# The heads' reciprocals of a three-stage language-model tower on one core: four transposes to 8 rows in place of one transpose to 32 rows and four masked copies

## What is computed

```python
h = relu(conv2(emb[ids]))                       # embedding and a two-tap filter
u = layernorm(h)
x_t = A x_(t-1) + B u_t                         # for 4 heads of 64, all t (a scan)
x = x / max_over_head(|x|) * exp(2)             # each token, each head
h = h + x @ C + u @ D
h = h + gelu(next(fc2_e(gelu(fc1_e(x_attn)))))  # x_attn = normed(h) @ attn + h, 8 experts
```

## Time and profile before

| | us |
|---|---|
| median of 3 runs | 210.72 (210.22 to 210.72) |
| span of the profiled execution, first to last instruction | 206.2 |
| PE busy | 181.0 |
| DVE busy | 143.2 |
| ACT busy | 116.5 |
| POOL busy | 97.5 |

### The profile page before, as it was taken

How to read it: one execution, slowest core, us unless ns; L and a number is a source line. 1 busy time by engine, 2 the same in 40 slices (tenths; PEclk the granted TensorE clock), 3 DMA queues, 4 the chain that set the end, 5 groups by cost and what they waited for, 6 DMA issues and landing times. The chain is left out here.

```text
span 206.2 us, 4072 instructions
## 1 busy us (share of the span) xinstructions
PE 181.0 (88%) x1407; PEld 163.3 (79%) x1407; DVE 143.2 (69%) x411; ACT 116.5 (56%) x317; POOL 97.5 (47%) x144
## 2 busy tenths in 40 slices
PE   0498999999999999999694999988979979996993
PEld 0276789999899987887594898987969969995891
DVE  1859956753444434669587685995977959569994
ACT  2037986554433355454444577847759577693771
POOL 0116644999200002239576184672843917656441
PEclk9999999999999999999999699999999999999999
DMA  5991000000000000000000000010100100010012
GB/s 137 399 423 62 3 0 5 2 0 3 0 0 3 0 0 2 3 0 0 0 3 2 0 3 0 0 51 5 51 0 3 52 0 27 27 51 2 3 52 102
DMA packets 2566, 7.60 MB, mean 37 GB/s; under 512 B 309, under 2 KB 1122, under 8 KB 2290
## 3 DMA queue, kind: packets, MB, share of 16 engines
q1 hardware_dynamic: 2258, 7.15, 9.1%
q10 hardware_dynamic: 288, 0.20, 0.4%
HBM read 5.25 MB, written 2.10 MB: 36 GB/s over the span
## 5 line engine op out<-in xcount | busy, mean ns | idle before, releaser
L421 POOL TENSOR_TENSOR hid_p<-hid_f,hid_p 128x256 fp32r<-128x256 f32 x56 | 40.2, 734 | 35.8 <-ACT hid_p L566 27.6
L564 ACT ACTIVATE hid_f<-bank,pa 128x256 f32<-128x256 f32 x64 | 30.3, 478 | 22.6 <-PE bank L1091 22.6
L1091 PE MATMUL bank<-xaT_p,fc_p 128*128 128x256 f32 x192 | 35.7, 297 | 0.8 <-ACT hid_f L564 0.7
L1111 PE MATMUL bank<-hid_p,out_hi 128*128 128x256 f32 x128 | 33.6, 288 | 0.6 <-POOL hid_p L421 0.5
L473 ACT ACTIVATE X<-bank 128x128 f32<-128x128 f32 x64 | 17.6, 279 | 23.3 <-PE bank L935 23.1
L1091 PEld LDWEIGHTS bank<-xaT_p,fc_p 128*128 128x128 f32 x192 | 27.3, 191 | 3.4 <-issue 2.0
L932 PE MATMUL bank<-uT,pa 128*128 128x128 f32 x128 | 25.1, 280 | 0.1
L843 DVE TENSOR_SCALAR xp<-h,mv,rstd 128x128 f32<-128x128 f32 x32 | 22.5, 762 | 3.3 <-POOL rstd L439 3.3
L1111 PEld LDWEIGHTS bank<-hid_p,out_hi 128*128 128x128 f32 x128 | 23.8, 188 | 1.2 <-POOL hid_p L421 0.9
L935 PE MATMUL bank<-X,pa 128*128 128x128 f32 x120 | 23.2, 275 | 0.0
L566 ACT ACTIVATE hid_p<-bank,pa 128x256 fp32r<-128x256 f32 x48 | 23.0, 478 | 0.0
(11 more groups left out here) (123 smaller groups left out, 384.4 us busy)
## 6 DMA issues: line engine op xcount, KB each, us to landing
fc_w<-in_fc SPq DMA_DIRECT2D x2, 2048.0 KB, 11.2
out<-res SPq DMA_DIRECT2D x7, 256.0 KB, 2.0
pb<-in_pack_b SPq DMA_DIRECT2D x1, 320.0 KB, 4.2
pa<-in_pack_a SPq DMA_DIRECT2D x1, 279.0 KB, 3.5
out<-res SPq DMA_DIRECT2D x2, 128.0 KB, 1.7
conv_w<-in_conv ACTq DMA_DIRECT2D x1, 128.0 KB, 3.4
pc<-in_pack_c ACTq DMA_DIRECT2D x1, 66.5 KB, 3.8
rowsel<-in_rows SPq DMA_DIRECT2D x1, 64.0 KB, 3.8
```

The lines of the kernel that those rows point to most:

```text
L421: nc.gpsimd.tensor_tensor(hid_p[1][:, half, c, :], hid_f[:, m % HID_SLOTS, :], hid_p[0][:, half, c, :].bitcast(F32), ALU.subtract).then_in ...
L564: full = nc.scalar.activation(hid_f[:, m % HID_SLOTS, :], src, ACT.Gelu, bias=bias)
L1091: last = mm(bank[5 + n % 2][:, 0:HALF], fc1_p[w][:, e * HID + c * P:e * HID + (c + 1) * P], xaT_p[m][:, b % 2, half, :], start=(k == 0), s ...
L1111: last = mm(out_bank(b, half)[:, half * HALF:(half + 1) * HALF], out_p[w][:, e, c * CH:(c + 1) * CH], hid_p[m][:, half, c, :], start=(c == ...
```

## The change

`r_s` gets the order (block, part, head) instead of (part, block, head), so that the 8 numbers of a block lie side by side. Each block is transposed by itself to 8 rows, into its own 128 columns of bank 4. Bank 4 then holds 8 rows by 512 columns, with no entry that has to be zeroed, and ACT takes it over with one plain copy. Before, one transpose gave 32 rows by 128 columns, and ACT wrote them four times, each time with a mask (`tile`, a scale for each partition) that kept the rows of one block. `sel_r` has 8 rows instead of 32, and the mask leaves `pack_c`.

```diff
-PC_COLS = dict(ident=P, iota=1, tile=NQ)
+PC_COLS = dict(ident=P, iota=1)
...
-        rcp = sb("rcp", [P, 2, NQ * NH])
-        r_s = sb("r_s", [P, 2, NS, NQ * NH])
-        r_T = sb("r_T", [NS * NQ * NH, 2, L], F32R)
+        rcp = sb("rcp", [P, 2, NQ, NH])
+        r_s = sb("r_s", [P, 2, NQ, NS, NH])
+        r_T = sb("r_T", [NS * NH, 2, L], F32R)
...
-        bank_rt = bank[4][0:NS * NQ * NH, 0:P]
+        bank_rt = bank[4][0:NS * NH, :]
...
-                            for q in range(NQ):
-                                mask = pc[0:NS * NQ * NH, PC["tile"]][:, q:q + 1]
-                                last = nc.scalar.activation(r_T[:, b % 2, q * P:(q + 1) * P], bank_rt, ACT.Copy,
-                                                            scale=mask)
-                            last.then_inc(rT_ready, 1)
+                            nc.scalar.activation(r_T[:, b % 2, :], bank_rt, ACT.Copy).then_inc(rT_ready, 1)
...
-                        hi = r_s[:, b % 2, 0, :]
-                        chained(nc.vector.tensor_scalar(hi.bitcast(F32R), rcp[:, b % 2, :], E2, None, ALU.mult))
-                        nc.vector.scalar_tensor_tensor(out=r_s[:, b % 2, 1, :], in0=rcp[:, b % 2, :], scalar=E2,
+                        hi = r_s[:, b % 2, :, 0, :]
+                        chained(nc.vector.tensor_scalar(hi.bitcast(F32R), rcp[:, b % 2], E2, None, ALU.mult))
+                        nc.vector.scalar_tensor_tensor(out=r_s[:, b % 2, :, 1, :], in0=rcp[:, b % 2], scalar=E2,
...
-                    nc.tensor.transpose(bank_rt, r_s[:, b % 2, :, :].rearrange("p s n -> p (s n)"),
-                                        ident).then_inc(rt_done, 1)
+                    for q in range(NQ):
+                        last = nc.tensor.transpose(bank_rt[:, q * P:(q + 1) * P],
+                                                   r_s[:, b % 2, q].rearrange("p s n -> p (s n)"), ident)
+                    last.then_inc(rt_done, 1)
```

More of the change, by code:

```diff
@@ L105, in build @@
         pb = sb("pb", [P, PB_N])
-        sel_r = sb("sel_r", [NS * NQ * NH, NP * P], F32R)
+        sel_r = sb("sel_r", [NS * NH, NP * P], F32R)
         fc1_p = [sb(f"fc1_p{s}", [P, NE * HID], F32R) for s in range(NS)]
@@ L182, in build @@
             attn_g = sb_early("attn_g", [P, CH])
-            sel_f = sb_early("sel_f", [NS * NQ * NH, NP * P])
+            sel_f = sb_early("sel_f", [NS * NH, NP * P])
         hid_p = [sb(f"hid_p{s}", [P, 2, HC, HALF], F32R) for s in range(NS)]
@@ L761, in _ @@
                         dve.wait_ge(amax_ready, b + 1)
-                        chained(nc.vector.reciprocal(rcp[:, b % 2, :],
-                                                     amax[:, b % 2, :, :].rearrange("p q n -> p (q n)")))
+                        chained(nc.vector.reciprocal(rcp[:, b % 2], amax[:, b % 2]))
                         if b >= 2:
                             dve.wait_ge(rt_done, b - 1)
-                        hi = r_s[:, b % 2, 0, :]
-                        chained(nc.vector.tensor_scalar(hi.bitcast(F32R), rcp[:, b % 2, :], E2, None, ALU.mult))
-                        nc.vector.scalar_tensor_tensor(out=r_s[:, b % 2, 1, :], in0=rcp[:, b % 2, :], scalar=E2,
+                        hi = r_s[:, b % 2, :, 0, :]
+                        chained(nc.vector.tensor_scalar(hi.bitcast(F32R), rcp[:, b % 2], E2, None, ALU.mult))
+                        nc.vector.scalar_tensor_tensor(out=r_s[:, b % 2, :, 1, :], in0=rcp[:, b % 2], scalar=E2,
                                                        in1=hi, op0=ALU.mult, op1=ALU.subtract).then_inc(rs_ready, 1)
@@ L1193 @@
     pack_b = np.concatenate([parts[n] for n in PB_COLS], 1)
-    tile = np.zeros((P, NQ), np.float32)
-    rows = tile[:NS * NQ * NH].reshape(NS, NQ, NH, NQ)
-    sel = np.zeros((NS, NQ, NH, NP, 2, DH), np.float32)
-    for q in range(NQ):
-        rows[:, q, :, q] = 1
+    sel = np.zeros((NS, NH, NP, 2, DH), np.float32)
     for n in range(NH):
-        sel[:, :, n, n // 2, n % 2, :] = 1
-    pack_c = np.concatenate([np.eye(P, dtype=np.float32), np.arange(P, dtype=np.float32)[:, None], tile], 1)
+        sel[:, n, n // 2, n % 2, :] = 1
+    pack_c = np.concatenate([np.eye(P, dtype=np.float32), np.arange(P, dtype=np.float32)[:, None]], 1)
     arrays = dict(
         ids=ids, emb=f(L0_tok_emb_weight), conv=f(L0_tok_conv_weight)[:, 0, :].T.reshape(1, 2 * CH),
-        pack_a=pack_a, pack_b=pack_b, sel=sel.reshape(NS * NQ * NH, NP * P),
+        pack_a=pack_a, pack_b=pack_b, sel=sel.reshape(NS * NH, NP * P),
         pack_c=pack_c, rows=np.repeat(np.eye(2 * NB, dtype=ml_dtypes.bfloat16), P, 1),
```

## The result

Over 20 runs of each, the changed kernel takes 211.22 us and the one before 210.47 (medians). The ratio is 1.0076, with a 95% interval of 1.0042 to 1.0110. The ratio gives + 1.6 us on 210.47, with + 0.9 to + 2.3 inside the interval: slower by about 1%, where + 1.9 was forecast. The runs of one kernel spread by more than the change is worth (208.07 to 211.80 and 209.70 to 214.78).

What follows compares the result with a forecast made beforehand. Rounds were taken as bound by two rings through PE's work after the reciprocals' transpose. Batches 2 to 7 + 1.98, batch 1 + 0.33, batch 0 - 0.38 give + 1.93 us: 212.6 us, whole range 211.2 to 213.7.

Steps and rivals of the forecast that it cites:

- The three transposes: Three added PE transposes per batch, taken as 0.11 us apart like other float32 ones: 0.33 us a batch.
- Four copies to one: ACT's copies of 1.11 us become one of 0.60, `r_T` ready 0.18 sooner; worth nothing from batch 1 on.
- Batch 0: The one place where the copies are on the path: L884 starts 0.38 us sooner, so - 0.38.
- Both rings: Dependency loops closing a round, over DVE and over POOL, both through PE after the reciprocals' transpose; each 0.33 us longer.
- The ring over DVE: Loop from the transpose of `r_s` over the transposes of `xa`, ACT's copy and DVE to the next `r_s`; 0.33 longer.
- the hold: DVE's L769 takes 0.70 us instead of 0.18 while POOL's subtraction runs, delaying `r_s` by 0.52; expected to stay.
- the copies release `xaT_p`: Rival: `xaT_p` waits for ACT's copies, so 0.18 us sooner in seven batches; - 1.6 us, 209.1; chance 0.05.
- the hold goes away: Rival: DVE's L769 is no longer slowed by POOL, saving up to 2.3 us, 210.3; chance 0.12.
- the other ring: Loop from the transpose over PE's matmuls, ACT's `hid_p` and POOL's subtraction, which slows DVE's L769; expected 0.33 us longer.
- From span to median: The 4.5 us between the profiled span of 206.2 and the median were taken to stay after the change.
- new holds: Rival: two more passes of DVE's L769 are slowed by POOL, 0.52 us each; + 1.0, 213.7; chance 0.11.

Runs made afterwards that it cites:

- experiment 1: Kernel before with its transpose of the reciprocals issued four times instead of once, the four masked copies kept; 1.0136 times the kernel before.
- experiment 2: Kernel before with one transpose and one unmasked copy of 32x512 in place of four masked copies, masking left out; 0.9943 times the kernel before.
- experiment 3: Changed kernel with its one copy of 8x512 cut into four plain copies of 8x128; 1.0082 times the kernel before.
- experiment 9: Kernel before with one more, unneeded matmul of 128x256 on PE in each of rounds 0 to 3; 0.9958 times the kernel before.
- experiment 10: Changed kernel with one more, unneeded matmul of 128x256 on PE in each of rounds 0 to 3; 1.0048 times the kernel before.
- experiment 8: Kernel before with one plain copy of 32x128 for four masked ones, and eight spreading matmuls of 128 columns for two of 512; 0.9954 times the kernel before.
- second profile: The changed kernel run again without any edit, on the same chip as the kernel before; 1.0080 times the kernel before, span 208.4 us.
- experiment 5: Changed kernel with 16 unread identity transposes filling PE's idle time before batch 3's wait for `r_s`; 1.0059 times the kernel before.

## Why the prediction was right

**The three transposes: right.** 0.11 us apart was taken; four take 0.60 us with 0.27 for one, (0.60 - 0.27) / 3 = 0.11. The eight weight columns make no difference: experiment 1 with 32 columns has 0.60 to 0.61 (and 1.01 once, in the window of the fallen clock). With the 56 ns of the Trainium skill, page "TensorE: Matmul & The Clock Gate", section "Wait — 56ns, not 53.3ns?", the sum would have been + 0.8 us, an estimate that lies just outside the measured + 0.9 to + 2.3. The rounds say 0.33 clearly.

**Four copies to one: right.** The copy takes 0.59 where 0.60 was taken. Its gain is nothing from batch 1 on (experiments 2 and 3). The price of the mask is now known: four copies of 128 columns take 1.11 us with it (32 rows) and 0.74 without (8 rows), 0.09 each. The Trainium skill, page "ScalarE: Activation LUTs", section "What ACT_TABLE_LOAD costs", gives about 93 ns for each per-partition operand (a scale or a bias with one value for each partition), and the runs agree.

**Batch 0: right.** The chain there was read from three rows. In the changed kernel:

```profile
76.94 0.60 PE L1014 MATMUL bank<-pc,r_s 128*8 128x128 f32 x4
...
77.58 0.59 ACT L575 ACTIVATE r_T<-bank 8x512 fp32r<-8x512 f32 x1
...
78.27 1.13 PE L878 MATMUL bank<-pb,fc_w 128*128 128x128 f32 x8
```

L878 comes 1.33 us behind the first transpose, against 1.72: - 0.39, where - 0.38 was forecast. It is carried whole to batch 1 (- 0.40).

**Both rings get longer by 0.33: right.** + 0.31 to + 0.33 in five intervals, and + 0.2 to + 0.3 from batch 7's transpose to the end of the span. The ring over DVE alone, without the hold, goes from 13.03 and 13.05 to 13.33 (experiments 9 and 10). PE's waits before batches 2 and 3 are 1.85 and 2.80 as before: idle time that was no cushion.

**Rival, the copies release `xaT_p`: refuted** for the kernel before by experiment 2, where a copy that is 0.5 us shorter gains nothing from batch 1 on. Experiment 3 and the eight recorded releases say the same of the changed kernel.

**Rival, the hold goes away: it did not happen, but it is real.** The hold stays in the changed kernel since both rings shift alike. Experiments 8, 9 and 10 show its price, 0.5 us a round, and that 0.12 us of work on the other ring decides it. Right in mechanism, as in "up to 0.52 each".

**From span to median: wrong, without weight for the time.** The prediction let the 4.5 us between the profile's span and the median stay. Of the executions that have both on record, each takes only 1.7 to 2.1 us more than its span, the changed kernel's profiled one 211.22 with a span of 209.4. So the execution with the span of 206.2 us took about 208 us, and some 2.7 of the 4.5 were the spread between executions. The + 1.9 and the 212.6 start from the median and stand without it. The forecast span of 208.1 does not: it came out as 209.4 and 208.4.

**Rival, new holds: in part; the clock had no term.** The profile has + 3.2 us of span and not + 1.9. Of that, 0.5 lie before batch 0 (76.94 against 76.46), and + 1.3 instead of + 0.3 from batch 3 to 4. PE's granted clock is below full there, the four transposes take 1.02 us instead of 0.60, and DVE's L762 is held once:

```profile
113.22 1.02 PE L1014 MATMUL bank<-pc,r_s 128*8 128x128 f32 x4 [2.80 <-DVE r_s L763]
...
127.42 0.55 DVE L762 TENSOR_SCALAR r_s<-rcp 128x16 fp32r<-128x16 f32 x1
```

In the kernel before, this round ended without a hold, and so did that of the changed kernel's second profile:

```profile
125.98 0.18 DVE L769 SCALAR_TENSOR_TENSOR r_s<-rcp,r_s 128x16 f32<-128x16 f32 x1
```

The profile of before had a fallen clock too. Its round of 13.70 is only 0.26 longer than the 13.44 of experiment 2, but that one has a hold of 0.38, so the fall cost about 0.64 us. In the changed kernel it cost 1.26 (experiment 5). Windows of 1 us show where it lay: in the changed kernel the granted clock is 0.74, 0.50, 0.50 and 0.56 from 112 to 116 us, and the transposes start at 113.22; in the kernel before it is 0.76, 0.50, 0.50 and 0.53 from 113 to 117, and the transpose starts at 112.51. So more of PE's work between the transposes and those of `xa`, through which both rings go, ran at the lower level. The two differences, 0.62 for the fall and 0.38 for the hold, make up the 1.0 by which the round exceeds the forecast. What sets the moment of the fall no run shows, nor whether the change moves it.

With the fall removed (experiment 5), the changed kernel has + 1.48 us from batch 0 to 7 against the 90.48 - 0.26 of before, a hold of 0.38 in both; the prediction's terms give 6 x 0.33 - 0.38 = + 1.6 there.

## What to carry to other kernels

Work moved from an idle engine's queue to a full one costs even if it saves more than it adds: ask first which of the two a round waits for. An idle time that ends with a wait is no room for work behind that wait; what stands behind it and does not need it belongs ahead of it, and that order was worth 3.5% where the edit itself cost 0.8. The worth of an edit is that of the order it stands in: in the last rounds the shorter copy was worth nothing in one order and 0.4 us a round in the other.

## What the runs showed of the hardware

- An instruction of 16 elements on DVE with two inputs in SBUF takes 0.17 us, or up to 0.74, if a POOL instruction on SBUF began a few hundredths of a microsecond before it. The one with a single input (L762 in the changed kernel) is held in the same way, for 0.55 us when POOL began 0.21 us before it. 0.12 us of unneeded PE work, by which the order of the two starts flipped, made rounds 0.5 us shorter.
- Eight matmuls of 128 columns whose operands are of type fp32r start 0.12 us apart, as those of 256 columns do (L1091 of the kernel before, three in 0.52 us with 0.28 for one). Below 256 columns they got no cheaper.
- A part of the spread from run to run may come from PE's start; no experiment tried it. In the changed kernel's first profile the groups of 16 bfloat16 matmuls, 1.05 us later on, take about 1.9 us twice, and then 1.37. In experiment 5's profile they take it at least four times, and batch 0's transpose starts at 79.04 instead of 76.94. The granted clock is recorded as 1.00 in those windows, so this slower start is seen only in the spacing of the matmuls:

```profile
10.30 1.89 PE L903 MATMUL bank<-tab,onehot 125*128 125x128 bf16 x16
...
16.26 1.37 PE L903 MATMUL bank<-tab,onehot 125*128 125x128 bf16 x16
```

```profile
10.40 1.89 PE L903 MATMUL bank<-tab,onehot 125*128 125x128 bf16 x16
...
20.21 1.91 PE L903 MATMUL bank<-tab,onehot 125*128 125x128 bf16 x16
```
